# First attention of a twelve-stage kernel: the softmax's subtraction and one wide exponential, or sixteen narrow exponentials with a bias

## What is computed

```python
_OFFSETS = list(range(41)) + [128, 48, 192]
idx = jnp.arange(T)[:, None] - deltas[None, :]
valid = idx >= 0
k_g = k[:, :, idxc]; v_g = v[:, :, idxc]
k_mod = k_g * (1.0 + scale_embed)
scores = jnp.einsum('bhtd,bhtjd->bhtj', q, k_mod) * scale
scores = scores + pos_bias.T[None, :, None, :]
scores = jnp.where(valid[None, None], scores, jnp.finfo(scores.dtype).min)
attn = jax.nn.softmax(scores, axis=-1)
out = jnp.einsum('bhtj,bhtjd->bhtd', attn, v_g)
```

## Time and profile before

| | |
|---|---|
| three executions | 3436.07, 3433.31, 3417.47 us; median 3433.31 us |
| the profiled execution | 3425.59 us, its span 3423.8 us |
| engines busy over the span | PE 3024.0 us (88%), DVE 2438.9 (71%), ACT 1801.9 (53%), POOL 856.2 (25%) |
| mean granted TensorE clock | 0.935 of full speed |

### The profile page before, as it was taken

How to read it: one execution, slowest core, us unless ns; L and a number is a source line. 1 busy time by engine, 2 the same in 40 slices (tenths; PEclk the granted TensorE clock), 3 DMA queues, 4 the chain that set the end, 5 groups by cost and what they waited for, 6 DMA issues and landing times. The chain is left out here.

```text
span 3423.8 us, 61642 instructions
## 1 busy us (share of the span) xinstructions
PE 3024.0 (88%) x24341; PEld 1632.8 (48%) x24381; DVE 2438.9 (71%) x5449; ACT 1801.9 (53%) x3292; POOL 856.2 (25%) x801
## 2 busy tenths in 40 slices
PE   4878579998799999998899879798997898898899
PEld 3434446566322222222566657476775232333677
DVE  8898588787699999993878853745335888883533
ACT  2223347677477777776778743133222466677221
POOL 0334147765100000001966710101203111212000
PEclk9899789999699999999999989899998689998999
DMA  1065221110410000000211110002003300000100
GB/s 53 9 156 121 83 62 35 36 35 13 157 77 1 1 2 1 1 1 19 71 26 36 32 31 1 11 19 75 25 1 88 98 32 1 35 2 1 48 1 13
DMA packets 77878, 129.19 MB, mean 38 GB/s; under 512 B 12772, under 2 KB 52616, under 8 KB 77384
## 3 DMA queue, kind: packets, MB, share of 16 engines
q1 hardware_dynamic: 77592, 125.25, 12.9%
HBM read 77.39 MB, written 34.19 MB: 33 GB/s over the span
## 5 line engine op out<-in xcount | busy, mean ns | idle before, releaser
L2007 ACT ACTIVATE AR<-ps 128x1024 f32<-128x1024 f32 (+2 forms) x756 | 717.7, 995 | 286.4 <-PE ps L1908 219.3
L2090 DVE TENSOR_REDUCE AR<-ps 128x1 f32<-128x512 f32 x1296 | 809.0, 683 | 48.5 <-PE ps L1877 47.4
L1908 PE MATMUL ps<-AR 32*128 32x512 bf16 (+3 forms) x4992 | 537.8, 378 | 9.3 <-ACT AR L2007 5.8
L1877 PE MATMUL ps<-AR 32*128 32x512 bf16 (+3 forms) x1664 | 478.6, 398 | 42.8 <-DVE AR L2090 13.5
L1925 PE MATMUL ps<-AR 128*32 128x512 f32 (+3 forms) x3328 | 439.4, 601 | 4.4 <-ACT AR L2012 3.9
L2499 PEld LDWEIGHTS ps<-AR 128*128 128x128 f32 x3072 | 364.8, 193 | 60.5 <-issue 47.4
L2658 DVE SCALAR_TENSOR_TENSOR X<-ps,AR,X 128x128 f32<-128x128 f32 x512 | 143.6, 344 | 344.7 <-PE ps L2499 344.3
L1877 PEld LDWEIGHTS ps<-AR 32*128 32x128 bf16 x1664 | 119.8, 92 | 549.7 <-DVE AR L2090 412.7
L2499 PE MATMUL ps<-AR 128*128 128x128 f32 x3072 | 364.9, 276 | 0.0
L2474 PE MATMUL ps<-XT,AR 128*128 128x512 f32 x672 | 307.7, 594 | 0.1
L1908 PEld LDWEIGHTS ps<-AR 32*128 32x128 bf16 x4992 | 185.2, 95 | 153.5 <-ACT AR L2007 48.7
(11 more groups left out here) (326 smaller groups left out, 4985.6 us busy)
## 6 DMA issues: line engine op xcount, KB each, us to landing
AR<-AR SPq DMA_DIRECT2D x124, 128.0 KB, 2.3
band<-AR SPq DMA_DIRECT2D x32, 450.0 KB, 5.1
AR<-band SPq DMA_DIRECT2D x32, 448.0 KB, 5.4
AR<-in_c_rot SPq DMA_DIRECT2D x64, 128.0 KB, 2.2
AR<-in_L3f_w SPq DMA_DIRECT2D x30, 256.0 KB, 5.4
rows_KA<-AR SPq DMA_DIRECT2D x32, 128.0 KB, 2.4
AR<-scr_bias SPq DMA_DIRECT2D x32, 128.0 KB, 3.2
AR<-in_L2f_w SPq DMA_DIRECT2D x30, 128.0 KB, 2.9
```

The source lines that it names most:

```text
L1877: e.matmul(g.bank[b][:, 0:w], QA[rows, q, 128 * i:128 * i + 128], KA[rows, q, 512 * first:512 * first + w], start=way != "kept", stop=True ...
L1908: t = e.matmul(g.bank[h][:, lo:512], K[32 * h:32 * h + 32, q, 128 * kt:128 * kt + 128], Q[32 * h:32 * h + 32, q, queries], start=y == 0, s ...
L2007: e.activation(dst[:, :, lo:512], src[:, :, lo:512], ACT.Exp, scale=self.scale).then_inc(*s.up("exp" if u else "left", k, i, *((1,) if u e ...
L2090: e.tensor_reduce(o, g.bank[b][:, 0:w], AXX, ALU.max).then_inc(*s.up("reduced", k, n, h, st, kc))
```

## The change

The subtraction on VectorE goes. The maximum is written negated, and ScalarE takes sixteen exponentials of 44 scores, one for each head, each with that head's negated maximum as its bias (one number for each partition, read from `mx`). ScalarE now waits for the maximum ("top") and no longer for the subtraction ("below"). The last of the sixteen raises "exp".

```diff
             if what == "exp":
-                e.wait_ge(*s.at("below", k, n))
-                e.activation(self.SM[:, j], self.SM[:, j], ACT.Exp).then_inc(*s.up("exp", k, n))
+                e.wait_ge(*s.at("top", k, n))
+                for h in range(16):
+                    t = e.activation(self.SM[:, j, h, :], self.SM[:, j, h, :], ACT.Exp, bias=self.mx[:, j, h:h + 1])
+                t.then_inc(*s.up("exp", k, n))
...
-                e.tensor_reduce(self.mx[:, j, :], self.SM[:, j], AXX, ALU.max).then_inc(*s.up("top", k, n))
-            if what == "exp":
-                e.wait_ge(*s.at("top", k, n))
-                e.tensor_tensor(self.SM[:, j], self.SM[:, j], bc(self.mx[:, j, :], [128, 16, NJ], 2),
-                                ALU.subtract).then_inc(*s.up("below", k, n))
+                e.tensor_reduce(self.mx[:, j, :], self.SM[:, j], AXX, ALU.max, negate=True).then_inc(*s.up("top", k, n))
```

## The result

| | before | changed |
|---|---|---|
| median of 22 runs | 3428.9 us (3417.5 to 3436.1) | 3438.15 us (3429.2 to 3445.7) |
| ratio | | 1.0026, 95% interval 1.0019 to 1.0033 |
| profiled execution, span | 3423.8 us | 3434.0 us |

The change costs 0.26%, 6.5 to 11.3 us: a real loss, though within the half per cent that I had called no change. It all lies in the stage. The table cuts the stage at the first lift of each chunk (the starts of the 128x512 addition, L752 and now L754, of tiles 0, 4, 8 and 12) and at its last addition (L784, now L782), and each chunk at its fourth sum (L768, now L766). All values are differences of starts in the two timelines.

A forecast was written before the change was run, and what follows sets the result against it. VectorE bounds each chunk while four tiles go through softmax, then TensorE. Chunks +1.0, +1.9, +1.9 and tail 0.0 sum to +4.8 us, set on a median of 3433.3: 3438 us, range 3421 to 3455.

The forecast's parts named there:

- one of my own signs: Stage's end: wrong if it moves by other than the three chunks' shifts; last addition some 5 us later.
- The price of the new instructions: ScalarE's sixteen biased 44-column exponentials: 330 ns each, pitch 0.22 us, 3.7 us a tile against 0.79 before.
- The first rival: Each tile's exponentials: pitch 0.34 us, 5.4 us a tile, ScalarE paces the softmax; +31 us, 3465; chance 0.13.
- the second (a bias for nothing): Each tile's exponentials: bias address free, 2.3 us a tile; total -12.7 us, 3421; chance 0.07.
- The tile's formula: Softmax of a tile: sum starts 4.66 us after the maximum's start, or when VectorE's products are done, whichever is later.
- Chunk 1 (+1.0): First chunk, tiles 0 to 3: shifts of +0.65, -0.56, +0.23 and +0.65 us, sum +1.0 us.
- The tail: Tiles 12 to 15: four subtractions saved, four longer exponentials in their place, 0.0 us.
- the waits in front of the sum that I named as signs: VectorE waits before the sum in all sixteen tiles, about 0.2 us behind six products, 1.4 to 2 us elsewhere.
- ScalarE's copies in front are held back by the copy L706: Tile 5, second chunk: copies some 0.15 us late, ending about 232.2; sum at 235.93, not 234.69, +1.24 in all.
- the clock falls for longer: Rival: VectorE's standstills idle TensorE, three stretches start at the lower clock, some 3.3 us each; +10, 3448; chance 0.10.
- The shift is absorbed: Rival: VectorE's idle 4.57 us before the third chunk's first lift absorbs the shift; only the tail counts, 3433; chance 0.08.
- I cost that at nothing: Score copies L692 up to 3 us later in tiles 6 and 7; buffers needed only two groups of offsets later.

The follow-up runs named there:

- e1: Kernel before, subtraction kept, with sixteen exponentials of 44 columns without a bias in place of the one of 704; ratio to before 1.0034, stage 228.04 us.
- e4: Changed kernel with GpSimd's far weights moved behind its next product in the first three chunks; ratio to before 1.0020, stage 222.55 us.
- e3: Changed kernel with two unread 512-column products on TensorE ahead of the gather that waits 3.17 us, in the last three chunks; ratio to before 1.0027, stage 223.57 us.
- e2: Kernel before with the subtraction left out and nothing in its place, one exponential waiting for the maximum; ratio to before 0.9953, stage 200.82 us.
- e9: Changed kernel with the norm due 0.145 after the lift and GpSimd's far weights 0.06 behind the norm; ratio to before 0.9980, stage 210.04 us.
- e10: Kernel before, subtraction and wide exponential kept, with the same two moves as e9; ratio to before 0.9974, stage 209.90 us.
- e7: Kernel before with the norm due 0.145 of a chunk after the lift, not 0.12, in the first three chunks; ratio to before 0.9984, stage 211.97 us.

## Why the prediction was right, and where it was not

**The median, 3438, and the range held**, but the match (3438.15) is luck, better than the working. Two misses cancel: I set the change on a median of 3433.3, which more runs put at 3428.9, and I had +4.8 us where the ratio says +8.9 (6.5 to 11.3) and the two stages +10.9. By one of my own signs I was wrong: the stage's end was to move by the three chunks' shifts alone, and these give 6.4 of the 10.9.

**The price of the new instructions was right.** I took 0.224 us a pitch, 330 ns each and 3.7 us a tile; measured 320 ns and sixteen in 3.66 to 3.69 us. (My rows give 0.22, from 0.33 less 0.11; the third digit does not follow from them.) With e1 the parts stand too: 0.13 without a bias, 0.09 for the bias. The first rival (a pitch of 0.34, 3465 us) and the second (a bias for nothing) are out. The Trainium skill's 0.3 us plus 0.83 ns an element ("ScalarE: Activation LUTs", rules for kernel authors) comes near for one such activation (320 ns against an estimate of 337); taken without an overlap, as in my first rival, it is 1.5 times too much for sixteen in a row (5.4 us against 3.66). The Trainium skill's warning against small SBUF operands ("VectorE: DVE Perf Modes", TRN2 errata) is borne out: 186 of the 223 ns in e1 don't depend on the columns, taken at 0.83 ns each.

**The tile's formula was right.** 4.66 us from maximum to sum: measured 4.62 to 4.64 in eight of the twelve tiles under products, and 5.1 in tiles 4 and 8, where ScalarE is late as reckoned. Chunk 1 (+1.0) came to +0.90 up to the fourth sum. The tail, which I put at 0.0 from saved subtractions against longer sets, came to -0.04, and by the steps worked out: its last exponentials end 17.0 us after tile 12's maximum starts, where I had 17.2. Of the waits in front of the sum that I named as signs, tile 14 has none, and tiles 2, 6 and 10 have 0.7 to 0.9 us, not 1.4 to 2.

**The step that failed first: "ScalarE's copies in front are held back by the copy L706 ... by some 0.15, and end at about 232.2".** I followed the wait through ScalarE and TensorE and did not ask who else waits for the sum of tile 4. GpSimd does, with a product queued behind it. That made tile 5's distance 6.21 and not 5.27 (235.93 - 230.66 of my working): 0.9 us in each of two chunks. e4 shows it.

**The second: "the clock falls for longer" was given 0.10 and left out of the sum.** It happened behind the second and third chunk, at 2.0 and 2.2 us (and 0.3 behind the first), where the rival had 3.3 for each of three. My own rows had what was needed: VectorE does four products in a row and then stands, so TensorE gets its gathers early and waits the longer for the next. In the changed kernel the last of tile 7's four products ends at 252.47 us and the next starts at 256.01; before, 251.85 and 253.96. e3 shows the cost, in the profiled executions; the medians are too coarse to part this step from the first. With 1.7 us from the first step (+2.75 for +1.9, twice) and 4.2 from this one the sum 4.8 becomes 10.7; the stages give 10.9.

**"The shift is absorbed"** is refuted by e2. "I cost that at nothing", of the score copies behind tiles 6 and 7, held: no gather of the stage waits for ScalarE, and those of the second chunk's end (row at 250.72) wait 1.34 us for VectorE's products, as before. The loss of 0.26% lies within the half per cent that I had called no change, but it is clear of the noise of 22 runs; my 17 us for what can be told was too coarse.

## What to carry to other kernels

Folding a subtraction into an activation's bias trades one wide instruction on VectorE for as many narrow ones on ScalarE as there are biases; count them at the measured pitch (0.224 us here) and set that against the work that stands between producer and consumer: where it is shorter, the other engine stands still and the gain turns into a loss (e1, the changed kernel); with more work in between the trade was about even here (e9 against e10). Before a wait is moved, list every engine that waits for the delayed step, with what is queued behind it there. And give the fed engine's idle time a line of its own: on TensorE a standstill that grew from 1.33 to 3.17 us was followed by some 2 us lost to the lower clock, because the work behind it was the bound.

## What I had not expected of the hardware

- The lower clock behind a short standstill, and that its place matters more than its being there. With 3.17 us in front of it a gather took 1.92 us, not 1.05, and 1.98 us of products that nobody reads brought it back to 1.04; before, the lower level lay ahead of the fourth sum and cost nothing. The same filling made no difference to the median that these runs could show; in its profile the clock stayed down longer in the tail.
- A product of 512 columns on VectorE takes 0.60 us a pitch alone; beside GpSimd's products the rows average 0.8 to 1.1 us, and unevenly: of two in a row that start with a GpSimd product the first took 0.60 and the second 1.50. Moving one product in front of the sum in each of the last two tiles of a chunk was worth 1.1 to 1.5 us a chunk in the kernel before (e7).
